# A four-layer transformer kernel: GpSimd's order of square roots and additions in the second layer's recurrence stage

## The chip, the cores and the metric

One core of a Trainium2 chip runs the whole program. The metric is the device time of one execution in microseconds (us). Before the change it is 2499.39 us, the median of 3 runs (2498.11 to 2508.93).

Engines are called PE (TensorE), ACT (ScalarE), DVE (VectorE), Pool (GpSimd) and SP (SyncE, which here only starts transfers). Each works through its own list of instructions in order and waits on semaphores where the list says so.

## What is computed

The reference applies four layers, each an attention-like part and a feed-forward part, to x of 8 sequences (B) of 100 rows (S) of 512 columns (D). The part in question is the attention-like part of the third one in the reference's counting (L2, called "the second layer" in the kernel's names, since two stand ahead of it in L0 and L1 and it has the class `SecondLayer`). Cut to what matters:

```python
# L2_xattn, called with Z = layernorm(x)
states = scan over kv of s = K * s + (kv @ W_in.T + b_in)
summary = mean over the rows of (states @ W_out.T + b_out)     # one vector of 512 per sequence
y = Z + summary
mu, var = mean and variance of y over its last axis
out = (y - mu) / sqrt(var + 1e-5) * gamma + beta
x = x + out
```

After it comes L2's feed-forward part: rows are normalized, rounded to an 8-bit format in blocks of 32, multiplied by gate and up weights, passed through silu, rounded again and multiplied by the down weights.

## The kernel before

The kernel is written engine by engine, in stages with a barrier between them. `stage_L2_recurrence` (L2874 to L3068) is one stage; `stage_ffn` (L2032) follows it as the next. The summaries are already there when the stage begins. The stage has two jobs that share the engines.

**The sequences.** All 8 sequences are held in `res` and are taken in the order 7, 0, 1, ... 6 (`ORDER`), called here by their position i = 0 to 7. For each, DVE does:

- `first(i)`: `measure` of res, that is mean and variance (L2954, L2955) and variance plus epsilon (L2956);
- `shifted(i)`: minus mean times reciprocal root (L2964), which ACT needs for `add_shift(i)` (L2933, summary plus shift);
- `second(i)`: y = res times root plus what ACT made (L2971), then `measure` of y;
- `third(i)`: (y minus mean) times gamma (L2980), then times the second root plus `rb` (L2982), which is the new res.

Pool computes both reciprocal roots of a sequence, `root` (L3021, one column to the power of minus a half), and `rb` = res + beta (L3029, 512 columns), called the addition here. `rb` has two buffers, so the addition for i waits until `third(i - 2)` has read the one it overwrites; that is the wait on `res_made` at L3028.

DVE's order in round i is: second(i), first(i + 2), third(i - 1), shifted(i + 2). After round 4 it also measures the last tile of rows (L2988 to L2990), and after round 5 it rounds that tile (L2995 and the helper `quantize_fp8`, L2007 to L2015). Pool's order is the list `roots`: (0,0), (1,0), then for each i the second root of i and the first root of i + 2; the addition for i comes right behind its first root. The last tile's root (L3032) stands behind the first root of i = 6.

**The weights.** SP loads 16 triples of weights, 768 KB each (L2917), into four buffers; triple t waits until PE has turned triple t - 4. PE transposes each in three banks (L3044) and computes the summaries' broadcasts in between (L3052); ACT copies the three banks out (L2943). ACT's `add_shift` for i = 1 to 7 stands in its list behind the copies of triples 0, 1, 4, 6, 8, 10 and 13 (`ADD_AT`), so ACT can be held by either job. Behind its last triple, SP writes the finished sequences into the tiles of the next stage (`into_tiles`, L1997), each after its `third`; sequence 7 (i = 0) goes out between triples 7 and 8.

At the end PE transposes the last tile (L3066), and after the barrier the feed-forward stage starts with that tile's gate and up products (L2134).

Of the kernel before, what the change touches and what calls it, by code (L numbers as in the profile page):

```python
# [12 lines left out]
ALU = mybir.AluOpType  # L13
# [4 lines left out]
B, S, D = 8, 100, 512  # L18
# [26 lines left out]
class Core:  # L45
# [22 lines left out]
    def sb(self, name, shape, dt=F32, ctx=None):  # L68
        return (ctx or self.ctx).enter_context(self.nc.sbuf_tensor(name, shape, dt))

    def sem(self, name):
        assert name not in self.names
        self.names.add(name)
        self.stage_sems.append(self.nc.alloc_semaphore(name))
        return self.stage_sems[-1]
# [2798 lines left out]
def stage_L2_recurrence(k, early, wgu, wd, rt, arrived, lead):  # L2874
# [5 lines left out]
    ORDER = [B - 1] + list(range(B - 1))  # L2880
    with ExitStack() as ctx:
        sb = lambda name, shape, dt=F32: k.sb("l2_" + name, shape, dt, ctx)
        sem = lambda name: k.sem("l2_" + name)
        gam, bet = early.gam, early.bet
# [8 lines left out]
        y, rb = [sb("y0", [S, D]), sb("y1", [S, D]), early.spare[5][0:S, :]], [sb(f"rb{i}", [S, D]) for i in range(2)]  # L2893
# [8 lines left out]
        var_made, rstd_made, y_made, rb_made, res_made, stepped = (  # L2902
            sem("var_made"), sem("rstd_made"), sem("y_made"), sem("beta_added"), sem("res_made"), sem("steps"))
# [6 lines left out]
        with nc.Block() as block:  # L2910

            @block.sync
            def _(sp):
                for t in range(2, FC):
                    if t >= 4:
                        sp.wait_ge(turned, 3 * (t - 3))
                    sp.dma_start(tri[t % 4][:], k.rounded[t]).then_inc(tri_in[t % 4], 16)  # L2917
                    if t == B - 1:
                        sp.wait_ge(res_made, 1)
                        into_tiles(k, sp, rt, ORDER[0], arrived)  # L2920
                for i, b in enumerate(ORDER[1:]):
                    sp.wait_ge(res_made, i + 2)
                    into_tiles(k, sp, rt, b, arrived)
# [93 lines left out]
            @block.gpsimd  # L3017
            def _(pool):

                def root(n):  # L3020
                    pool.tensor_tensor(rstd[:, n:n + 1], var[:, n:n + 1], k.half[0:S, :], ALU.pow).then_inc(rstd_made, 1)  # L3021

                for at, (i, which) in enumerate(roots):
                    pool.wait_ge(var_made, at + 1)
                    root(2 * i + which)
                    if which == 0:
                        if i >= 2:
                            pool.wait_ge(res_made, i - 1)  # L3028
                        pool.tensor_tensor(rb[i % 2][:], k.res[:, ORDER[i], :], bet[:], ALU.add).then_inc(rb_made, 1)  # L3029
                    if (i, which) == (B - 2, 0):  # L3030
                        pool.wait_ge(x_var_made, 1)
                        pool.tensor_tensor(x_rstd[:], x_var[:], k.half[0:m_last, :], ALU.pow).then_inc(x_rstd_made, 1)  # L3032

            @block.tensor
            def _(pe):
# [35 lines left out]
def stage_L2(k, early, third, weights):  # L3071

    with ExitStack() as ctx:
        wgu = k.sb("s2_wgu", [P, KC, 2 * FF], F32, ctx)
        wd = k.sb("s2_wd", [P, FC, D], F32, ctx)
        rt = k.sb("s2_rows", [P, len(TILES), D], F32, ctx)
        arrived = [k.sem(f"s2_tile{t}") for t in range(len(TILES))]
        third_in = k.sem("s2_third_in")
        lead = k.sb("s2_lead", [P, 1, KC, P], F32, ctx)
        stage_L2_recurrence(k, early, wgu, wd, rt, arrived, lead)  # L3080

        def prefetch(sp):
            for dst, src in zip([third.last, *early.kv, third.ctx[:]], weights):
                sp.dma_start(dst, src).then_inc(third_in, 16)
            return (third_in, 6 * 16),

        stage_ffn(k, "f2", wgu[:, :, 0:FF], wgu[:, :, FF:2 * FF], wd[:], rt,
                  [(a, 16 * len(tile_pieces(t))) for t, a in enumerate(arrived)], quantize_fp8, BLOCK, begin=prefetch, lead=lead[:])
# [847 lines left out]
```

## Time and profile before

| what | value |
|---|---|
| median of 3 runs | 2499.39 us |
| the profiled execution, its own time | 2497.65 us |
| its span | 2495.9 us |
| PE busy | 2368.1 us (95%) |
| DVE busy | 1345.6 us (54%) |
| ACT busy | 786.3 us (32%) |
| Pool busy | 729.7 us (29%) |
| stage_L2_recurrence, about | 1591 to 1652 us of the span |

Times in the views count from the start of the span. A start and a duration stand first; what is in square brackets is the time that the engine stood idle before the instruction, and what ended it. The shares of the whole span say little about a stage of 61 us: each engine's waits have to be read from the stage's own window.

### The profile page before, as it was taken

The numbers are of one execution on the slowest core, as the hardware profiler recorded it, in microseconds if no ns is written. First come the engines' busy times: TensorE is split into PE (matmuls) and PEld (weight loads), VectorE is DVE, ScalarE is ACT, GpSimd is POOL, SyncE is SP. The second block draws the span as 40 slices with busy tenths as digits, with TensorE's granted clock in tenths as the row PEclk, the third lists the DMA queues.
The fourth block names the chain that finished last, engine by engine and source line by source line (L and its number), as shares of the span: only waits on it lengthen the run. The fifth ranks groups of instructions, "written<-read, shape, count | busy, mean of one in ns | idle before, by whom it ended". The sixth has DMA issues, their size and how long they took to land. (4 is left out here: it accounts for less than half of the span.)

```text
span 2495.9 us, 30147 instructions
## 1 busy us (share of the span) xinstructions
PE 2368.1 (95%) x10329; PEld 1276.0 (51%) x10329; DVE 1345.6 (54%) x3448; ACT 786.3 (32%) x2069; POOL 729.7 (29%) x728
## 2 busy tenths in 40 slices
PE   8999999989999998999979999879999899999899
PEld 4455455556355555555555555534444344444454
DVE  5544344126111324767667777676664355565797
ACT  1134444204011113555541010321110255655433
POOL 3655455204100004311133334310000165665200
PEclk9999999999999998999959999989999899999799
DMA  7026200014285543110043222530000321210100
GB/s 192 1 80 218 88 17 8 0 46 141 81 293 206 194 142 87 51 35 30 1 154 132 98 82 99 207 140 6 4 9 4 111 58 47 55 47 28 37 13 15
DMA packets 93678, 203.31 MB, mean 81 GB/s; under 512 B 18580, under 2 KB 37428, under 8 KB 91864
## 3 DMA queue, kind: packets, MB, share of 16 engines
q1 hardware_dynamic: 87384, 188.26, 22.5%
q0 software_dynamic: 6144, 13.13, 1.9%
q8 instruction: 85, 1.39, 0.2%
q14 instruction: 65, 0.53, 0.1%
HBM read 150.45 MB, written 45.94 MB: 79 GB/s over the span
## 5 line engine op out<-in xcount | busy, mean ns | idle before, releaser
L3638 POOL TENSOR_SCALAR a_p<-a_p,a_li 100x257 f32<-100x257 f32 x252 | 188.4, 771 | 110.3 <-DVE a_li L3501 110.3
L633 POOL TENSOR_SCALAR a_shared<-a_shared,a_li 128x361 f32<-128x361 f32 x104 | 131.8, 1267 | 182.3 <-DVE a_li L541 182.3
L3256 PE MATMUL bank<-l_early,a_ctx 128*128 128x512 f32 (+1 forms) x384 | 180.0, 614 | 0.0
L2560 PE MATMUL bank<-s_xT,s_w 128*128 128x400 f32 x512 | 179.0, 504 | 0.8 <-PEq L2757 0.8
L2560 PEld LDWEIGHTS bank<-s_xT,s_w 128*128 128x128 f32 x512 | 98.1, 192 | 77.1 <-issue 3.9
L1853 POOL DMA_INDIRECT a_got<-slots_y,slots_of x32 | 33.8, 1057 | 318.6 <-POOLq L1193 309.8
L3256 PEld LDWEIGHTS bank<-l_early,a_ctx 128*128 128x128 f32 (+1 forms) x384 | 68.8, 188 | 85.0 <-issue 84.9
L313 PE MATMUL bank<-a_wk,a_ctx 128*128 128x512 f32 (+1 forms) x192 | 95.2, 616 | 9.7 <-DMA a_wk<-in_L_xattn_Wk 6.1
L691 ACT ACTIVATE a_shared<-a_shared,a_nm 128x361 f32<-128x361 f32 x104 | 62.1, 597 | 99.5 <-DVE a_nm L535 99.5
L2355 ACT ACTIVATE f_sg<-bank 128x512 f32<-128x512 f32 x25 | 14.9, 597 | 241.4 <-PE bank L2138 221.7
L2570 PE MATMUL bank<-f_h,s_w 128*128 128x400 f32 x256 | 90.9, 499 | 0.0
L313 PE MATMUL bank<-a_wv,a_ctx 128*128 128x512 f32 (+1 forms) x192 | 90.7, 592 | 0.0
L2629 ACT ACTIVATE f_sg<-bank 128x400 f32<-128x400 f32 x32 | 16.1, 504 | 236.2 <-PE bank L2560 236.2
L396 PE MATMUL bank<-a_q_o,a_wq_wo 128*128 128x400 f32 x256 | 88.4, 500 | 0.6 <-issue 0.6
L1284 PE MATMUL bank<-e_wd,e_midT 128*128 128x512 f32 (+1 forms) x192 | 87.9, 593 | 0.6 <-ACT e_midT L1321 0.6
L2164 PE MATMUL bank<-s_wd,f_hT 128*128 128x512 f32 x192 | 87.1, 598 | 0.0
L1546 PE MATMUL bank<-w_wv,w_ctx 128*128 128x512 f32 (+1 forms) x192 | 87.0, 597 | 0.0
L328 PE MATMUL bank<-a_wq_wo,a_shared 128*128 128x512 f32 x192 | 86.5, 593 | 0.0
L1538 PE MATMUL bank<-w_ctx,w_wk 128*128 128x361 f32 x256 | 86.1, 480 | 0.0
L2138 PE MATMUL bank<-s_wgu,f_xT 128*128 128x512 f32 x192 | 84.6, 593 | 0.7 <-ACTq L2345 0.7
L2138 PE MATMUL bank<-s_wgu,s_lead 128*128 128x512 f32 x192 | 84.4, 592 | 0.0
L1341 DVE TENSOR_TENSOR e_mid<-e_sg,bank 128x352 f32<-128x352 f32 x32 | 16.7, 521 | 125.1 <-PE bank L1264 125.1
(477 smaller groups left out, 4964.3 us busy)
## 6 DMA issues: line engine op xcount, KB each, us to landing
slots_x<-zero SPq DMA_DIRECT2D x4, 4096.0 KB, 27.0
f_triple<-in_L_ffn_triples SPq DMA_DIRECT2D x16, 768.0 KB, 4.3
rounded<-f_triple SPq DMA_DIRECT2D x16, 768.0 KB, 3.3
s_whole<-in_L_ffn_w SPq DMA_DIRECT2D x24, 512.0 KB, 3.7
e_wg<-in_L_ffn_w_gate SPq DMA_DIRECT2D x16, 704.0 KB, 4.5
e_wu<-in_L_ffn_w_up SPq DMA_DIRECT2D x16, 704.0 KB, 6.5
e_wd<-in_L_ffn_w_down SPq DMA_DIRECT2D x16, 512.0 KB, 4.1
e_xg<-slots_x SPq DMA_DIRECT2D x16, 512.0 KB, 5.3
```

What stands on the lines that cost most here:

```text
L313: mm = nc.tensor.matmul(R.bank(name, b, c)[0:m, :], cx[:, kc, lo:lo + m], w[:, kc, :], start=(kc == 0), stop=(kc == KC - 1))
L328: mm = nc.tensor.matmul(bank[:], xnT[:, kc, t * P:(t + 1) * P], wq[:, kc, n * D:(n + 1) * D], start=(kc == 0), stop=(kc == KC - 1))
L396: mm = nc.tensor.matmul(R.bank("y", half, m)[:, 0:BY_HALF * S], wo[:, h, m * P:(m + 1) * P], qo[:, half * BY_HALF:(half + 1) * BY_HALF, h, ...
L633: pool.tensor_scalar(p[s % NP], p[s % NP], li[:, b % 2, h:h + 1], None, ALU.mult).then_inc(normed, 1)
L1284: mm = nc.tensor.matmul(b_y[:], midT[u % 2][0:n, c, :], wd[e % 2][0:n, c, :], start=(c == 0), stop=(c == len(IC) - 1))
L1546: mm = nc.tensor.matmul(R.bank("v", b, c)[0:m, :], cx[b % 2][:, kc, lo:lo + m], wvs[:, kc, :], start=(kc == 0), stop=(kc == KC - 1))
L2138: mm = nc.tensor.matmul(banks[u % 2][:], xT[i % 2][:, n, kc, :], w[:, kc, j * D:(j + 1) * D], start=(kc == 0 and n == 0), stop=(kc == KC - ...
L2164: mm = nc.tensor.matmul(b_y[i % 2][:], hT[u % 2][:, n, kc, :], down[:, j * KC + kc, :], start=(j == 0 and kc == 0 and n == 0), stop=(j == ...
L2560: mm = nc.tensor.matmul(banks[f % 2][:, 0:GT], w[:, kc, f * P:(f + 1) * P], xT[:, kc, :], start=(kc == 0), stop=(kc == KC - 1))
L2570: mm = nc.tensor.matmul(b_y[d][:, 0:GT], down[:, f, d * P:(d + 1) * P], h[f % 2][:], start=(f == 0), stop=(f == FC - 1))
L3256: mm = nc.tensor.matmul(bank[0:m, :], columns[:, kc], w[:, kc, :], start=(kc == 0), stop=(kc == KC - 1))
L3638: pool.tensor_scalar(p[g % 2][j][:, lo:hi], p[g % 2][j][:, lo:hi], li[:, h, i:i + 1], None, ALU.mult) \
```

## The change

Pool now takes the second root of i and the first root of i + 2 one after the other, and only then does an addition: the one for i + 1 instead of i + 2. The first two additions stay where they were; the last one stands between the two last roots. The additions, their waits and the number of instructions stay the same.

```diff
+                def add_beta(i):
+                    if i >= 2:
+                        pool.wait_ge(res_made, i - 1)
+                    pool.tensor_tensor(rb[i % 2][:], k.res[:, ORDER[i], :], bet[:], ALU.add).then_inc(rb_made, 1)
+
                 for at, (i, which) in enumerate(roots):
                     pool.wait_ge(var_made, at + 1)
                     root(2 * i + which)
-                    if which == 0:
-                        if i >= 2:
-                            pool.wait_ge(res_made, i - 1)
-                        pool.tensor_tensor(rb[i % 2][:], k.res[:, ORDER[i], :], bet[:], ALU.add).then_inc(rb_made, 1)
+                    if which == 0 and i < 2:
+                        add_beta(i)
+                    elif which == 0 and i >= 3:
+                        add_beta(i - 1)
                     if (i, which) == (B - 2, 0):
                         pool.wait_ge(x_var_made, 1)
                         pool.tensor_tensor(x_rstd[:], x_var[:], k.half[0:m_last, :], ALU.pow).then_inc(x_rstd_made, 1)
+                    if (i, which) == (B - 2, 1):
+                        add_beta(B - 1)
```

## Rows read from the trace of the kernel before

**Rows 1.** The page, part 1: busy time of each engine over the span.
```profile
PE 2368.1 (95%) x10329; PEld 1276.0 (51%) x10329; DVE 1345.6 (54%) x3448; ACT 786.3 (32%) x2069; POOL 729.7 (29%) x728
```

**Rows 2.** Waits from 1588 to 1668: who waited for whom, total, times, longest.
```profile
POOL l_rb L3029 <- DVE res L2982: 32.5, 6, 8.9
...
DVE l_shift L2964 <- POOL l_rstd L3021: 13.2, 6, 2.9
```

**Rows 3.** DVE's timeline in the recurrence stage: start, duration, engine, line, operation.
```profile
1595.52 1.52 DVE L2971 SCALAR_TENSOR_TENSOR l_y<-res,l_rstd,l_early 100x512 f32<-100x512 f32 x1 [0.76 <-ACT l_early L2933]
...
1603.56 0.75 DVE L2982 SCALAR_TENSOR_TENSOR res<-l_y,l_rstd,l_rb 100x512 f32<-100x512 f32 x1
1606.73 0.16 DVE L2964 SCALAR_TENSOR_TENSOR l_shift<-l_stat,l_rstd 100x1 f32<-100x1 f32 x1 [2.42 <-POOL l_rstd L3021]
1606.81 0.74 DVE L2971 SCALAR_TENSOR_TENSOR l_early<-res,l_rstd,l_early 100x512 f32<-100x512 f32 x1
...
1610.39 0.75 DVE L2982 SCALAR_TENSOR_TENSOR res<-l_y,l_rstd,l_rb 100x512 f32<-100x512 f32 x1
...
1627.23 0.67 DVE L2988 BATCH_NORM_STATS2 l_x_stats<-s_rows 32x6 f32<-32x512 f32 x1
...
1628.21 0.73 DVE L2971 SCALAR_TENSOR_TENSOR l_early<-res,l_rstd,l_early 100x512 f32<-100x512 f32 x1
...
1635.44 0.16 DVE L2964 SCALAR_TENSOR_TENSOR l_shift<-l_stat,l_rstd 100x1 f32<-100x1 f32 x1 [2.91 <-POOL l_rstd L3021]
...
1643.46 0.75 DVE L2982 SCALAR_TENSOR_TENSOR res<-l_early,l_rstd,l_rb 100x512 f32<-100x512 f32 x1
1644.13 0.75 DVE L2971 SCALAR_TENSOR_TENSOR l_y<-res,l_rstd,l_early 100x512 f32<-100x512 f32 x1
...
1645.86 0.15 DVE L2956 TENSOR_SCALAR l_var<-l_stat 100x1 f32<-100x1 f32 x1
1646.54 0.75 DVE L2980 SCALAR_TENSOR_TENSOR l_y<-l_y,l_stat,l_early 100x512 f32<-100x512 f32 x1 [0.53 <-POOL l_rstd L3021]
...
1648.78 0.75 DVE L2982 SCALAR_TENSOR_TENSOR res<-l_y,l_rstd,l_rb 100x512 f32<-100x512 f32 x1
```

**Rows 4.** Pool's timeline in the same stage.
```profile
1595.23 1.26 POOL L3029 TENSOR_TENSOR l_rb<-res,l_early 100x512 f32<-100x512 f32 x1
...
1604.39 1.28 POOL L3029 TENSOR_TENSOR l_rb<-res,l_early 100x512 f32<-100x512 f32 x1 [4.52 <-DVE res L2982]
1605.62 1.07 POOL L3021 TENSOR_TENSOR l_rstd<-l_var,half 100x1 f32<-100x1 f32 x2
...
1644.30 1.70 POOL L3029 TENSOR_TENSOR l_rb<-res,l_early 100x512 f32<-100x512 f32 x1 [8.89 <-DVE res L2982]
```

**Rows 5.** ACT's timeline: the last copy of triple 8, and add_shift(5).
```profile
1617.89 0.60 ACT L2943 COPY s_wd<-bank 128x512 f32<-128x512 f32 x1
...
1620.54 0.69 ACT L2933 ACTIVATE l_early<-bank,l_shift 100x512 f32<-100x512 f32 x1 [2.05 <-DVE l_shift L2964]
```

**Rows 6.** PE's timeline: triple 8, and the next stage's first products.
```profile
1616.23 1.53 PE L3044 MATMUL bank<-ident,l_early 128*128 128x128 f32 x12 [2.28 <-DMA l_early<-rounded]
...
1652.07 9.37 PE L2134 MATMUL bank<-s_wgu,s_lead 128*32 128x512 f32 x64 [10.61 <-PEq L2910]
```

**Rows 7.** Five us in mid-stage: PE, PEld, DVE, ACT, POOL busy, PEclk, DMA share, GB/s.
```profile
1615.00:1620.00 5.00, 3.77 (x26) 2.82 (x27) 2.78 (x8) 2.44 (x5) 1.97 (x3) 1.00 1.01 381
```

**Rows 8.** SP's timeline: finished sequences into the tiles of the next stage.
```profile
1625.80 25.48 SPq L1997 DMA_DIRECT2D s_rows<-res  x12
```

**Rows 9.** The third layer's timeline, Pool's root beside DVE's products.
```profile
1974.73 0.74 POOL L3651 TENSOR_TENSOR a_rstd<-a_var,half 100x1 f32<-100x1 f32 x1
...
1974.32 2.33 DVE L3477 SCALAR_TENSOR_TENSOR a_k<-a_k,a_kr,a_nk 128x512 f32<-128x512 f32 x3 [0.17 <-POOL a_kr L3643]
```

**Rows 10.** The next stage's first products in two windows: PE, PEld busy, PEclk, DMA share, GB/s.
```profile
1652.07:1656.70 4.63, 4.63 (x24) 1.33 (x28) 0.50 0.73 242
1656.70:1661.40 4.70, 4.70 (x44) 1.22 (x36) 1.00 1.01 427
```

## The prediction

> **What bounds the kernel now.** I read the shares first: PE is busy 95% of the span [rows 1], so over the whole kernel time is won by shortening stretches in which PE isn't. The recurrence stage is one: ahead of the next stage's first products PE stood idle 10.61 us [rows 6]. What PE waits for there is the stage's end, so I read next who waits inside the stage. Two entries of the list of waits form a ring [rows 2]: Pool waited 32.5 us in six pieces for DVE's finished res before its additions, and DVE waited 13.2 us in six pieces for Pool's roots before the shift. The timelines show the ring turning. DVE starts the last product of a sequence at 1603.56 and ends it at about 1604.31; Pool's addition starts at 1604.39, 0.08 later, and behind it stand two roots, 1605.62 and on for 1.07; only when the second is done does DVE go on, at 1606.73, after 2.42 us idle [rows 3, 4]. The inputs of both roots were there before the addition began: Pool's own order held them up. The same pattern stands four times with 2.40 to 2.42, once with 2.91 (at 1635.44, where the last tile's root stands in Pool's list too), and the first of the six waits, 13.2 - 2.91 - 4 x 2.4 = 0.7, is ahead of the ring and stays. From res of the last sequence (1648.78 + 0.75 = 1649.53) to the next stage (1652.07) it is 2.54 us [rows 3, 6], in which SP sends the last pieces [rows 8]. So DVE's chain ends the stage.
>
> **The change part by part.** No instruction is added or removed. Three things move.
>
> *Both roots ahead of the addition, rounds 1 to 5.* The inputs come before third(i - 1), which takes DVE 0.75 + 0.75 with its gaps; two roots take 1.07 [rows 4], the first of them a good 0.9 earlier than the second. So both are ready when DVE reaches the shift and its wait goes to nothing. Without a wait, DVE starts the next instruction 0.67 after the start of the last product (1643.46 to 1644.13), and second follows the shift by 0.08 [rows 3]. A round from second to the last product takes 3.58 (1606.81 to 1610.39), so a round costs 3.58 + 0.67 + 0.08 = 4.33 instead of 6.81. Pool's work in a round is 1.26 + 1.07 = 2.33 and fits [rows 4].
>
> Starting from 1603.56: shift at 1604.23, second(2) at 1604.31, second(3) at 1608.64, second(4) at 1612.97. Round 4 ends with the measurement of the last tile, 1628.21 - 1627.23 = 0.98 [rows 3], so second(5) would start at 1612.97 + 4.33 + 0.98 = 1618.28.
>
> *What is late next.* second(5) needs add_shift(5), which ACT has behind the copies of triple 8. PE waited for that triple's transfer until 1616.23 [rows 6], and there the DMA engines were busy throughout (share 1.01) [rows 7], so it won't come earlier. ACT's last copy of it starts at 1617.89; a next instruction follows after about 0.47 us, at 1618.36, and add_shift takes 0.69 [rows 5], so second(5) starts at about 1619.08. That is a new wait of 0.8 us. Before, it started at 1628.21: gained so far 9.13.
>
> *Rounds 5 to 7.* The wait of 2.91 before the shift goes, with 0.07 for the restart: 2.98. The rounding of the last tile, second(6) and third(5) cost what they did. Then, at 1646.54, DVE waited for the second root of i = 6, because Pool had the last addition ahead of it [rows 3, 4]. Now that root is done before. Third(6) can start right behind the variance op, 0.07 after 1645.86, instead of at 1646.54: gained 0.61. The last addition now stands between the two last roots. It takes 1.70 from 0.09 after res, as it does now, and ends about when the last variance is there, so it costs nothing; third(6)'s 1.5 us of products cover the last root.
>
> *The queues passed.* Pool issues no DMA in this stage. SP's transfers of finished sequences stand behind the last triple in its list whatever Pool does [rows 8]; four sequences will be done by then instead of three to four, and SP needs some 0.8 us for each piece, done by about 1630, ahead of the last three sequences. The tail of 2.54 stays.
>
> *Collisions.* Before, five of the additions in the ring ran while DVE stood idle. Now each runs beside second. The trace shows both outcomes. At 1644.30 an addition came 0.17 after the start of second: DVE kept its 0.75 and the addition took 1.70 instead of 1.26. At 1595.52 second came 0.29 after an addition had started and took 1.52 instead of 0.75 [rows 3, 4]. In the new rounds second starts 0.09 ahead of the addition (at the end of res; Pool follows 0.08 or 0.09 later). That is on the side of the first case, so I take nothing for DVE; the upper bound is 1.2 in each of rounds 1, 2, 3 and 5 (DVE held to the addition's end, as at 1595.52, where it ended 1.81 after Pool's start instead of 0.65), less the 0.8 that the new wait would swallow. The Trainium skill, SBUF — State Buffer, "SBUF: two separate sides", speaks against this change: a GpSimd instruction and a VectorE instruction with two SBUF inputs share a port pair under an exclusive lock, and whichever starts first holds it for its whole instruction. By it the sum stays if VectorE counts as first, and falls by the upper bound if GpSimd does; the two stretched rows agree with it.
>
> The root of i + 2 now runs beside third's products. Beside three such products back to back (2.33 us together, so none was stretched) a root took 0.74 instead of some 0.55 [rows 9]. The root slips between two of them: 0.2 later, covered by the second product. In round 5 the addition meets the first instructions of the rounding: bounds 0 and one addition, 1.26; I take 0.1, since small one-input instructions beside an addition, such as the one at 1645.86, keep their 0.15.
>
> *The next stage.* It starts after idle time of PE in both kernels, at a granted clock of 0.50, that is 1.2 GHz, for 4.63 us, then 2.4 GHz [rows 10]. The idle time ahead shrinks (some 7 instead of 10.61 us), so it may start otherwise. Bounds: half of 4.63 less, or half clock also over the second window, 4.70 more. I take no difference, the row itself.
>
> **Sum:** 9.13 + 2.98 + 0.61 - 0.1 = 12.6 us. Against the profiled execution's 2497.65 that makes 2485.0; the median of the runs is 1.7 above it, so 2499.39 - 12.6 = 2486.8. A measurement of this kernel can tell about 0.5% from no change, 12.5 us: the forecast lies on that line.
>
> **The rivals.**
>
> *A, collisions go Pool's way.* Price as above: rounds 1 to 3 lose 3 x 1.16 - 0.8 = 2.7, round 5 about 0.7; gain 9.2, time 2490.2. For it: the margin is only 0.09 us, and DVE's instruction is then still behind the shift in its pipe. Against: the order of the starts. The skill's lock, cited above, is the same mechanism.
>
> *B, the stream of weights becomes the bound.* ACT's add_shift waits behind copies of triples that arrive no faster; if the copies slip by another 1.5 us around triples 8 to 10, or triple 13's by as much, the wait of 0.8 grows to 2.3: gain 11.1, time 2488.3. For it: the DMA share of 1.01 [rows 7]. Against: those transfers are asked for at the same times as before.
>
> *C, the change doesn't do what it says.* If the second root were starved by third's products and the shift still came after the addition, nothing would be won: 2499.4. Rows 9 speak against it.
>
> *D, slower.* If Pool's addition and roots held DVE's second and both products of third, each for a whole addition, a round would lose 3 x 1.26 = 3.8 and win 2.5: five rounds 6.5 us more, 2505.9. It decides from 2.5 us lost a round. The largest stretch in these rows is 0.77 for one instruction.
>
> **How the numbers follow.** Forecast 0.68, A 0.20, B 0.08, C 0.02, D 0.02. The forecast's own range is 2485 to 2488 (1 us for the next stage's clock, 1 for the measurement). The range 2484.3 to 2490.9 adds A and B. Faster by over 0.5% is a little over half of the forecast's share, for a clock that can also give: 0.40. D's price is under 0.5%, slower by over 0.5% gets 0.01; the rest, 0.59, is within 0.5%.
>
> **What would show it.** DVE's waits for l_rstd before the shift: only the first (0.7) left; second(2), (3), (4) 4.33 apart; second(5) behind ACT at about 1619.1 with a wait of 0.8 on l_early; Pool's additions 1.70 to 1.8 long in rounds 1 to 3 with second at 0.75 (under A: additions 1.26 and second 1.5 to 1.9); roots of 0.7 beside third; PE's first products of the next stage at about 1639.5. It is wrong if the rounds are over 5 us apart, if that start comes after 1643, or if it comes there and the kernel's time doesn't follow.

## The result, and the profile after

The changed kernel took 2494.24 us in the median of 12 runs (2486.83 to 2496.72), the kernel before beside it 2500.41 us (12 runs). The ratio is 0.9965, 95% interval 0.9954 to 0.9977: 8.7 us of 2500, faster, but less than the 12.6 forecast, and the median lies outside the range given. Measured twice more, beside other kernels, the changed kernel came to 2490.43 us (0.9954, 0.9940 to 0.9967) and 2490.82 us (0.9960, 0.9946 to 0.9973).

The stage itself shows what the change did without the noise of the rest. From DVE's first instruction in it (the copy into `l_each`, at 1591.32 before) to the next stage's first product (1652.07, [rows 6]) it took 60.75 us. In the changed kernel's profile it runs from 1595.21 to 1649.04: 53.83 us, a gain of 6.92 where 12.6 was forecast. The profiled execution's own time fell from 2497.65 to 2495.03 only, because the preceding feed-forward part was 3.6 us longer in this execution. That part is untouched by the change and took 276 to 277 or 280 to 281 us from one execution to the next, of either kernel. The thirteen profiled executions with the longer time had a stretch of 6.8 us in it at a granted clock of 0.50 (here from 1449.4 to 1456.2), the five with the shorter one had none.

Who waited, 1580 to 1660, after the change. These rows answer to [rows 2]:

```profile
POOL l_rstd L3021 <- DVE l_var L2956: 27.9, 12, 7.2
...
DVE l_y L2971 <- ACT l_early L2933: 4.6, 2, 3.8
...
POOL l_rb L3026 <- DVE res L2982: 2.8, 6, 0.5
...
DVE l_early L2971 <- ACT l_early L2933: 2.4, 1, 2.4
...
DVE l_shift L2964 <- POOL l_rstd L3021: 0.7, 1, 0.7
```

The ring is open. DVE's 13.2 us for Pool's roots are down to the 0.7 that the prediction left standing, and Pool's 32.5 us for res to 2.8. In their place DVE waits for ACT: 3.8 and 2.4 us for `add_shift`, and 0.8 at the start, which stood before too [rows 3].

DVE's timeline after; compare [rows 3]:

```profile
1607.45 0.75 DVE L2982 SCALAR_TENSOR_TENSOR res<-l_y,l_rstd,l_rb 100x512 f32<-100x512 f32 x1
1608.12 0.15 DVE L2964 SCALAR_TENSOR_TENSOR l_shift<-l_stat,l_rstd 100x1 f32<-100x1 f32 x1
1608.19 0.74 DVE L2971 SCALAR_TENSOR_TENSOR l_early<-res,l_rstd,l_early 100x512 f32<-100x512 f32 x1
...
1612.44 0.15 DVE L2964 SCALAR_TENSOR_TENSOR l_shift<-l_stat,l_rstd 100x1 f32<-100x1 f32 x1
1616.39 0.75 DVE L2971 SCALAR_TENSOR_TENSOR l_y<-res,l_rstd,l_early 100x512 f32<-100x512 f32 x1 [3.80 <-ACT l_early L2933]
...
1620.71 0.74 DVE L2971 SCALAR_TENSOR_TENSOR l_y<-res,l_rstd,l_early 100x512 f32<-100x512 f32 x1
...
1628.50 0.75 DVE L2971 SCALAR_TENSOR_TENSOR l_early<-res,l_rstd,l_early 100x512 f32<-100x512 f32 x1 [2.42 <-ACT l_early L2933]
...
1634.10 0.42 DVE L2008 TENSOR_SCALAR l_x_top<-l_x_top 32x16 f32<-32x16 f32 x1
...
1645.73 0.75 DVE L2982 SCALAR_TENSOR_TENSOR res<-l_y,l_rstd,l_rb 100x512 f32<-100x512 f32 x1
```

A round without a wait is 4.32 us (shift to shift, 1608.12 to 1612.44) and the restart is 0.67, as forecast. second(3) then stands from 1612.5 to 1616.39, and second(5) until 1628.50.

Pool's timeline, one round of it; compare [rows 4]:

```profile
1606.84 0.99 POOL L3021 TENSOR_TENSOR l_rstd<-l_var,half 100x1 f32<-100x1 f32 x1 [0.46 <-DVE l_var L2956]
1608.29 1.77 POOL L3026 TENSOR_TENSOR l_rb<-res,l_early 100x512 f32<-100x512 f32 x1 [0.46 <-DVE res L2982]
1610.15 0.55 POOL L3021 TENSOR_TENSOR l_rstd<-l_var,half 100x1 f32<-100x1 f32 x1
```

Pool now pays for the collisions (its instructions that overlap DVE's), out of time that it has. The root beside third's products takes 0.99 instead of 0.55 and is still done before the shift; the addition beside second takes 1.77, and second keeps its 0.74.

PE's timeline shows what ACT waits for, and the windows under it the clock (their columns are PE, PEld, DVE, ACT, POOL busy, PEclk, DMA share, GB/s):

```profile
1608.61 5.08 PE L3051 MATMUL bank<-ident,l_triple 128*128 128x128 f32 x24
...
1622.92 2.82 PE L3051 MATMUL bank<-ident,l_early 128*128 128x128 f32 x12 [0.78 <-DMA l_early<-rounded]
1625.67 2.02 PE L3059 MATMUL bank<-l_summaries,l_each 8*100 8x512 f32 x2
```
```profile
1596.30:1613.20 16.90, 16.90 (x54) 10.82 (x53) 14.15 (x36) 7.75 (x14) 10.06 (x12) 0.50 0.54 191
1613.30:1620.00 6.70, 5.95 (x45) 4.62 (x44) 3.40 (x9) 6.55 (x13) 1.76 (x3) 1.00 0.95 295
1620.20:1630.20 10.00, 9.22 (x36) 6.94 (x35) 7.23 (x18) 5.36 (x9) 5.22 (x6) 0.50 0.90 352
```

For 17 us from the stage's start the granted clock was 0.50 (1.2 GHz), with PE busy every one of them, and again for 10 us from 1620. Twelve transposes of one triple, 1.53 us at full clock [rows 6], took 2.82, and a summary's products 2.02 instead of 1.10. In the kernel before's profile the clock was back at 1.00 7.4 us after the stage's start. So triple 4, behind which add_shift(3) stands in ACT's list, was laid out after 1615; triple 8, behind which add_shift(5) stands, was turned from 1622.92 instead of 1616.23, 27.7 us into the stage instead of 24.9.

The last thing that ACT waited for ahead of add_shift(5) was not a copy, though, but the summary's product behind triple 8 (1625.67 + 2.02 = 1627.69). ACT's row after, and PE's row of that product in the kernel before:

```profile
1627.78 0.69 ACT L2933 ACTIVATE l_early<-bank,l_shift 100x512 f32<-100x512 f32 x1 [1.42 <-PE bank L3059]
```
```profile
1617.69 1.10 PE L3052 MATMUL bank<-l_summaries,l_each 8*100 8x512 f32 x2
```

The transfers moved too. SP asked for triple 8 at 1606.72 before, 15.4 us into the stage, and at 1615.52 after, 20.3 us into it:

```profile
1606.72 1.52 SPq L2917 DMA_DIRECT2D l_early<-rounded  x2
```
```profile
1615.52 1.20 SPq L2917 DMA_DIRECT2D l_early<-rounded  x2
```

That is one execution. Two theories can be made of it. Theory 1: the stream of weights through PE and ACT is the new bound, and how much it takes back hangs on what the clock happens to do. Theory 2: the stage always gives 7 us and the forecast missed a fixed cost.

### The profile page after: what moved, and what is told of

Its sections match the earlier page's. It is cut to its first block and busy times, and to the rows that moved or that the text cites. A ratio compares the mean times of both kernels' runs of the same rounds, so it can differ in the third digit from the quotient of the medians.

```text
span 2493.3 us, 30147 instructions
## 1 busy us (share of the span) xinstructions
PE 2377.4 (95%) x10329; PEld 1284.9 (52%) x10329; DVE 1345.9 (54%) x3448; ACT 786.8 (32%) x2069; POOL 733.4 (29%) x728
## 3 DMA queue, kind: packets, MB, share of 16 engines
q8 instruction: 85, 1.39, 0.2%
```

## The experiments

Stages are measured as above, in the one profiled execution of each run. "Half clock" is how long the granted clock stood at 0.50 after it fell at the stage's start.

**e1, e11, e15: the changed kernel again, three more executions.**

> The changed kernel once more. In the first look its recurrence stage (from DVE's first instruction to the next stage's first product) took 53.8 us against 60.8 before, with PE at half clock from 1596.5 to 1613.6, and DVE waited 3.8 and 2.4 us for add_shift. Theory 1 (the stream of weights through PE and ACT is the new bound, and how late it is hangs on when PE's granted clock is 0.5): another execution shows another pattern of half clock, and the stage's length follows it: near 48 us where the clock is full early, 52 to 56 where it is half for 10 us or more; ratio 0.995 to 0.998. Theory 2 (the stage always gives 7 us, the rest never existed because of collisions of Pool and DVE): 53.8 within 0.3 us whatever the clock does, second over 0.75 us long somewhere.

> The changed kernel a third time, for one more pair of clock pattern and stage length. Theory 1: half clock for 10 us at the start gives 50.0 as in the second look, 17 us gives 53.8 as in the first, 7 us gives 48.4 to 49.5.

> The changed kernel a fourth time, on the same chip as the two others, as their measure: ratio 0.995 to 0.9970, stage 48.5, 50.0 or 53.8 us for 6.8, 10.2 or 17.1 us of half clock at its start.

| profiled execution of the changed kernel | half clock | second stretch of it | second(3), second(5) waited | stage |
|---|---|---|---|---|
| first | 17 us | 10 us | 3.80, 2.42 | 53.83 |
| e15 | 13.6 us | 10 us | 2.21, 4.08 | 53.89 |
| e1 | 10.2 us | 3.4 us | 0.74, 1.38 | 50.04 |
| e11 | 6.8 us | 3.4 us | none, 1.00 | 48.50 |

The wait of second(5) in DVE's timeline, e11 and then e15:

```profile
1622.01 0.75 DVE L2971 SCALAR_TENSOR_TENSOR l_early<-res,l_rstd,l_early 100x512 f32<-100x512 f32 x1 [1.00 <-ACT l_early L2933]
```
```profile
1627.45 0.75 DVE L2971 SCALAR_TENSOR_TENSOR l_early<-res,l_rstd,l_early 100x512 f32<-100x512 f32 x1 [4.08 <-ACT l_early L2933]
```

and the windows of e11's and of e15's clock (columns as above):

```profile
1594.60:1601.20 6.60, 6.55 (x17) 3.53 (x18) 5.60 (x13) 1.89 (x4) 3.76 (x5) 0.50 0.60 240
1601.40:1614.90 13.50, 11.48 (x78) 8.28 (x77) 12.15 (x32) 11.68 (x23) 8.47 (x10) 1.00 0.83 276
```
```profile
1596.00:1609.40 13.40, 13.40 (x43) 8.40 (x42) 11.43 (x28) 6.65 (x11) 8.04 (x10) 0.50 0.59 220
...
1619.90:1629.90 10.00, 8.43 (x32) 6.16 (x31) 5.64 (x14) 5.10 (x9) 3.79 (x5) 0.50 0.76 300
```

The stage's length follows the clock from execution to execution over 5.4 us; theory 2 is out. Without the two waits the four stages are alike: 47.61, 47.60, 47.92 and 47.50 us in the table's order, and 0.33 of e1's 47.92 is a second(3) of 1.08 us instead of 0.75 beside an addition. The clock at the start also moves the request for triple 8: 20.3, 18.6, 17.0 and 15.4 us into the stage. The expectations named only the first stretch and gave 48.5, 50.0 or 53.8 for it; e15 shows that the second counts too: 13.6 us of the first and 10 of the second gave as much as 17 and 10. With the clock early at full, as it was in the profile that the forecast was made from, the stage was 48.50 where 60.75 - 12.6 = 48.15 was forecast. The mean over the four stages is a gain of 9.2 us; the three ratios are 8.7, 11.5 and 10.0 us.

**e2: the kernel before again.**

> The kernel before once more, for a second look at its stage. Theory 1: Pool's wait of 2.4 us a round gives the stream of weights slack, so the stage stays at 60 to 62 us even where PE's clock is half for longer than in the first look, and the waits of DVE for the root stay 2.4. Theory 2 says the same of the length.

2501.61 us, and a stage of 60.75 us, the same to 0.01, with half clock for 17 us:

```profile
1596.00:1612.90 16.90, 16.90 (x58) 11.59 (x57) 12.46 (x31) 8.77 (x15) 6.88 (x9) 0.50 0.59 210
```
```profile
POOL l_rb L3029 <- DVE res L2982: 32.5, 6, 8.9
...
DVE l_shift L2964 <- POOL l_rstd L3021: 13.2, 6, 2.9
```

The waits are those of [rows 2] to the last digit. The 2.4 us that DVE lost to Pool in each round were slack for the weights, enough for either clock. This is why the profile before couldn't show how the stream does when nothing gives it slack.

**e4: PE's share of the stream cut.** Only the first of four blocks of each part is transposed; the other columns of the weights are what the bank held.

```diff
-                        for kc in range(KC):
+                        for kc in range(1):
```

> The changed kernel, but PE transposes only the first of the four 128-column blocks of each part of a triple; the other three parts of the weights are left as the bank held them, so this leaves out three quarters of the transposes. Theory 1: PE's clock no longer matters to the stage, only the transfers do: no wait for add_shift over 1 us, stage 47.5 to 49 us, that is the forecast's 12.6 us; ratio 0.994 to 0.996. Theory 2: stage 53 to 54 us still. A third, that the transfers alone are the bound (share 1.01 in mid-stage): stage 52 to 54 us too, but with DVE's waits on add_shift kept while PE waits for DMA.

Stage 47.58 us; ratio 0.9931 (0.9913 to 0.9949). DVE never waited for add_shift after the first, though the clock was at half for all of it:

```profile
1597.70:1643.70 46.00, 30.15 (x67) 11.50 (x65) 40.12 (x91) 29.00 (x57) 25.07 (x25) 0.50 0.78 271
```

So the clock matters to the stage through PE's transposes. All transfers are still there in e4, and PE could start on triple 8 at 1618.30, 22.1 us into the stage, where e11 had 24.6: the transfers by themselves don't make DVE wait either.

**e10: no transfers of triples 4 to 15.** What they would bring is left out of the weights.

```diff
-                    sp.dma_start(tri[t % 4][:], k.rounded[t]).then_inc(tri_in[t % 4], 16)
+                    if t < 4:
+                        sp.dma_start(tri[t % 4][:], k.rounded[t]).then_inc(tri_in[t % 4], 16)
...
-                    if t >= 2:
+                    if 2 <= t < 4:
                         pe.wait_ge(tri_in[t % 4], 16 * (t // 4 + (t % 4 >= 2)))
```

> The changed kernel without the transfers of triples 4 to 15; PE turns what the buffers hold already, so the wrong weights are laid out and this leaves out three quarters of the loading. If transfers alone delay add_shift: no wait of DVE for it, 47.6. If PE and ACT at half clock do: waits of 0.5 to 3.5 us stay, stage 49 to 52, longer the longer the clock is half. With the clock full early: 47.6.

Half clock was 6.8 us here, as in e11, and the stage 47.69 us against e11's 48.50, with no wait of DVE for add_shift but the one at the start. Beside e11, the transfers cost 0.8 us. But it takes both jobs to make that wait, since e4, with all transfers and a quarter of the transposes, hasn't got it either: a triple is asked for when PE has turned the one four before it. The two executions also differ in the clock, which fell a second time at 20.9 us into e11's stage and not before 38.2 us in e10's. e10 was profiled once, with a short stretch of half clock; what the transfers cost with a long one stays open.

**e3: add_shift one triple earlier.**

```diff
-        ADD_AT = [0, 1, 4, 6, 8, 10, 13]
+        ADD_AT = [0, 1, 3, 5, 7, 9, 12]
...
-                    elif t >= 6 and t % 2 == 0 and t // 2 + 1 < B:
-                        summary(t // 2 + 1)
+                    elif t >= 5 and t % 2 == 1 and (t + 3) // 2 < B:
+                        summary((t + 3) // 2)
```

> The changed kernel with ACT's add_shift for i = 3 to 7 behind triples 3, 5, 7, 9, 12 instead of 4, 6, 8, 10, 13, and the summaries' products on PE moved along. Theory 1: DVE's waits for add_shift fall by a triple each, some 2 us for the one behind triple 4, nearly all of the others; stage 49 to 52 us; 1 to 4 us faster than the changed kernel, ratio to before 0.9945 to 0.997. Theory 2: stage and time as the changed kernel's, ratio 0.9965.

2488.68 us, ratio 0.9946 (0.9932 to 0.9960), beside e1's 0.9954. The stage was 47.60 us, under the 49 to 52 expected, with 10.2 us of half clock; e1 had the same clock at the start and 50.04. Both waits of DVE are gone. e3's clock didn't fall a second time before 45.8 us into the stage, as e1's did for 3.4 us, but that isn't what saved them: PE came to triple 8 at 26.3 us into the stage in e3 and at 26.2 in e1. What was new is that add_shift(5) no longer stood behind it:

```profile
1622.21 0.92 DVE L2971 SCALAR_TENSOR_TENSOR l_early<-res,l_rstd,l_early 100x512 f32<-100x512 f32 x1
```

**e7: the same edit on the kernel before.**

> The kernel before with ACT's add_shift one triple earlier, the edit that took the changed kernel's stage from 50.0 to 47.6. Theory 1: before the change DVE never waited for add_shift in these rounds, since Pool held it longer, so nothing moves: stage 60.75 within 0.1, ratio 0.999 to 1.001. Rival: the edit helps by itself, 58 to 60.

Stage 60.73 us with 17 us of half clock, ratio 1.0004 (0.9995 to 1.0013): nothing. What costs 2.4 us in the changed kernel (e1 beside e3, one execution each) cost nothing in the one before. The position of add_shift became a bound by the change.

**e6: the last addition's part alone.**

```diff
-                    if which == 0:
-                        if i >= 2:
-                            pool.wait_ge(res_made, i - 1)
-                        pool.tensor_tensor(rb[i % 2][:], k.res[:, ORDER[i], :], bet[:], ALU.add).then_inc(rb_made, 1)
+                    if (which == 0 and i < B - 1) or (i, which) == (B - 2, 1):
+                        n = i if which == 0 else B - 1
+                        if n >= 2:
+                            pool.wait_ge(res_made, n - 1)
+                        pool.tensor_tensor(rb[n % 2][:], k.res[:, ORDER[n], :], bet[:], ALU.add).then_inc(rb_made, 1)
```

> The kernel before with one part of the change alone: the addition for i = 7 stands behind the second root of i = 6. Forecast for this part: 0.61 us of the stage's 60.75, so 60.1; DVE's wait of 0.53 ahead of third(6) gone, the five waits of 2.4 to 2.9 left. Rival: 60.75 still, because the second root of i = 7 comes late in its place.

60.12 us: 0.63 for the 0.61 of the sum.

**e5: the order left, a third buffer instead.**

```diff
-[sb(f"rb{i}", [S, D]) for i in range(2)]
+[sb(f"rb{i}", [S, D]) for i in range(3)]
...
-                        if i >= 2:
-                            pool.wait_ge(res_made, i - 1)
-                        pool.tensor_tensor(rb[i % 2][:], k.res[:, ORDER[i], :], bet[:], ALU.add).then_inc(rb_made, 1)
+                        if i >= 3:
+                            pool.wait_ge(res_made, i - 2)
+                        pool.tensor_tensor(rb[i % 3][:], k.res[:, ORDER[i], :], bet[:], ALU.add).then_inc(rb_made, 1)
```

> The kernel before in its own order, but with three buffers for res + beta instead of two, so that the addition for i waits for third(i - 3) and not third(i - 2). If the wait of the addition on the finished res is the cause, and the order only a way around it: DVE's waits for l_rstd in rounds 1 to 5 go to nothing here too, stage 48 to 52 us as far as add_shift lets it, ratio 0.994 to 0.997, like the changed kernel. If the order itself matters (roots behind an addition of 1.26 us, and collisions with third), some 0.5 to 1 us a round stays.

Stage 49.96 us with half clock for 10.2 us and then 3.4 more, where e1 had the same and 50.04; ratio 0.9967 (0.9954 to 0.9980). The wait on a finished res in front of the roots was the cause; the order is one way around it, a buffer another. Only the start differs, where an addition came before a shift:

```profile
1603.87 1.22 DVE L2964 SCALAR_TENSOR_TENSOR l_shift<-l_stat,l_rstd 100x1 f32<-100x1 f32 x1 [0.66 <-POOL l_rstd L3021]
```

**e8 and e16: additions where DVE runs only statistics.** With e3's edit; Pool's loop becomes

```diff
+                    if which == 1 and 1 <= i < B - 1:
+                        pool.wait_ge(y_made, i + 1)
+                        add_beta(i - 1 if i < B - 3 else i)
                     pool.wait_ge(var_made, at + 1)
                     root(2 * i + which)
-                    if which == 0 and i < 2:
-                        add_beta(i)
-                    elif which == 0 and i >= 3:
-                        add_beta(i - 1)
                     if (i, which) == (B - 2, 0):
+                        pool.wait_ge(res_made, B - 4)
+                        add_beta(B - 4)
```

> The changed kernel with the earlier add_shift (47.60 us of stage) and the additions placed where DVE runs only statistics: each behind second (a wait on y_made) instead of behind the first roots or third. If a port held by one engine at a time explains the stretched instructions (shift(0) 0.95 instead of 0.15, second(0) 1.52 instead of 0.75, the small scaling 0.43 instead of 0.16, second(5) 0.92 instead of 0.75), all of them fall to the short values: 0.8 + 0.77 + 0.27 + 0.17 = 2.0 less, stage 45.6; ratio 0.993 to 0.995. If the long values have another cause (first use of a tile, ACT's output arriving), they stay and the stage is 47.6 or longer.

> e8's kernel again on the same chip: is its gain over the changed kernel (stage 47.05 against 48.5 to 53.8) seen in the whole time? Expected ratio 0.9935 to 0.9955, 1 to 5 us under the changed kernel; stage 46 to 48 whatever the clock does, since add_shift stands a triple earlier.

The long instructions at the start became short, as the port theory says. e8's timeline of DVE, compare 1595.52 in [rows 3]:

```profile
1594.22 0.15 DVE L2964 SCALAR_TENSOR_TENSOR l_shift<-l_stat,l_rstd 100x1 f32<-100x1 f32 x1
1595.13 0.75 DVE L2971 SCALAR_TENSOR_TENSOR l_y<-res,l_rstd,l_early 100x512 f32<-100x512 f32 x1 [0.76 <-ACT l_early L2933]
...
1599.59 0.75 DVE L2971 SCALAR_TENSOR_TENSOR l_y<-res,l_rstd,l_early 100x512 f32<-100x512 f32 x1 [0.68 <-ACT l_early L2933]
```

The small scaling fell to 0.16 too; only second(5), beside the addition left in round 4, kept 0.92. Yet the stage was 47.05 and 47.07 us, 0.5 less than e3's and not 2.0: the third row above shows the won time turning into waits for add_shift again (0.68 and 0.30 in e8, 1.10 in e16), early in the stage where PE is at half clock in every execution. In the whole time: 2488.97 us, 0.9952 (0.9935 to 0.9968), and 2487.87 us, 0.9949 (0.9934 to 0.9963), beside e15's 0.9960; 3 us of median, and the intervals overlap.

**e9: a real product ahead of each triple.**

```diff
+                        if i == 0:
+                            nc.tensor.matmul(t_bank[n % 4][:], k.ident[:], k.zero[:], start=True, stop=True)
```

> The changed kernel with one real product ahead of each triple's transposes: the identity times 512 columns of zeros into the bank that the transposes then overwrite. It adds 16 products to PE. So far the clock stayed at 0.50 for 10 to 17 us at the start of the stage although PE was busy all the time with transposes. Theory 1: if products and not transposes bring the clock to 1.00, the half-clock stretch ends after some 7 us, DVE's waits for add_shift fall to what the transfers leave (0.8 as forecast, up to 1.4), stage 48.4 to 49.5 us, that is the forecast's 48.1 and 0.26 for the one collision seen. Rival: PE is only loaded further and the clock does as before, stage 50 to 54.

The clock was at half for 6.8 us and then at full for 44, with no second stretch, which the changed kernel had in all four executions:

```profile
1603.50:1647.70 44.20, 39.92 (x226) 26.39 (x224) 36.71 (x78) 28.05 (x54) 19.06 (x19) 1.00 0.75 248
```

The added product isn't shown to be what kept it there: without one, and with add_shift a triple earlier, e3, e8 and e16 had no second stretch for 34 to 38 us either. And the stage was 53.41 us all the same. The expectation had left out the price, which PE's timeline shows:

```profile
1609.78 1.02 PE L3051 MATMUL bank<-zero,ident 128*128 128x512 f32 x2
1610.64 1.47 PE L3053 MATMUL bank<-ident,l_triple 128*128 128x128 f32 x12
```

A triple took PE 2.17 us (1609.78 to 1611.95) instead of 1.4, and PE was the bound at full clock too. Ratio 0.9968 (0.9954 to 0.9982).

**e13: the product ahead of the first two triples only.**

```diff
+                        if i == 0 and t < 2:
```

> The changed kernel with the added product of zeros ahead of the first two triples alone. e9, with 16 of them, had its clock at 0.50 for only 6.8 us, but 1.0 us more PE work a triple made PE the bound (53.4). If products at the start are what ends the half-clock stretch early, it is 6.8 us here too, and with 14 products less the stage is 48.5 to 50, the two products costing up to 2 us each at half clock ahead of triples 0 and 1. If it was chance in e9 and e12, 10 or 17 us of half clock can come again, with 50 to 56.

Half clock 6.8 us again; stage 50.44, above the 48.5 to 50 expected, ratio 0.9956 (0.9939 to 0.9973). The products, at half clock themselves, hold triples 0 and 1, and second(1) waits 0.48 for it. Another 0.44 of waiting at second(3) let Pool's addition come first, and second took 1.39 instead of 0.75. second(5) waited 1.23 for add_shift, with the clock at full from 8.5 to 42.6 us into the stage.

**e12 and e14: all edits together,** e8's kernel with the product ahead of all 16 triples and ahead of two.

> The kernel of e8 (earlier add_shift, additions beside statistics) with the products of e9. e8's stage was 47.05, with waits of 0.76, 0.68 and 0.30 for add_shift at its start. If these are PE at half clock, the later two go and the stage is 46.0 to 46.5; ratio 0.9925 to 0.9955, at or below any other here. If the added products delay the summaries more than the clock gives back, 47 or more.

> e8's kernel (earlier add_shift, additions beside statistics) with the product ahead of the first two triples. Stage 46 to 48.5 us: e8's 47.05 with 0.68 + 0.30 of waits to win, and up to 2 us of product in front of triple 1. Ratio 0.9925 to 0.9955.

Ratios 0.9938 (0.9926 to 0.9950), 2486.31 us, and 0.9936 (0.9922 to 0.9949), 2485.32 us: the two lowest ratios of kernels that compute everything, e14 5.5 us of median under the changed kernel on the same chip. Their stages don't explain that: 50.56 and 48.33 us, longer than e8's 47.05. What else they win, if it is not chance, stays open. In both, second(1) waited 2.3 us for add_shift(1) behind the added products.

Half clock at the start was 6.8 us in all four executions with an added product, but also in e10, e11, e16 and the first of the kernel before, which have none. The records show what else goes with it. In those four without a product the clock fell 0.45 to 0.72 us after the stage's start; in the other ten without one it fell 0.96 to 1.79 us after it and stayed down for 10 us or more. Three of the four with a product fell late too (1.20 to 1.63) and yet had 6.8 us. So the products seem to matter where the fall is late. Three executions don't settle it, and no run here shows why.

## Why the prediction was right and wrong

- **The ring of Pool and DVE, rounds 1 to 5:** right in mechanism and size. DVE's waits for the shift went from 13.2 us to 0.7, rounds without a wait are 4.32 us (4.33 forecast), and e5 reaches the same stage by a buffer.
- **Rounds 5 to 7, the last addition:** right, 0.63 us alone (0.61).
- **The queues passed and the tail:** right. From the last res (1645.73 + 0.75 = 1646.48) to the next stage (1649.04) it is 2.56 us (2.54), although SP came to its last 12 pieces only 39.4 us into the stage, later than the "done by about 1630" of the prediction (38.7).
- **The next stage's first products:** right, with no difference taken: 9.61 us after and 9.37 before.
- **Collisions:** the side was right, rival A is out. Where they started on time, second(2), second(3) and second(4) kept 0.74 to 0.75 (all three in e11), in the first execution 0.09 to 0.10 ahead of the addition. A second that came after the addition had begun was stretched: 1.08 for second(3) in e1, and 0.92 for second(5) in e3, e10 and e8, where it didn't wait and the addition of round 4 runs while DVE measures the last tile. The prediction had no term for round 4; in the changed kernel second(5) waited in all four executions, and it cost nothing. By the lock of the Trainium skill, "SBUF — State Buffer", section "SBUF: two separate sides", whichever of the two engines starts first keeps the port pair; the trace agrees in both directions: the addition took 1.77 when second was first, the shift 1.22 in e5 when the addition was. Two sizes were off: the root beside third takes 0.99, not 0.7 (covered), and the small scaling in round 5 0.42 instead of 0.16, so 0.26 us where 0.1 was taken.
- **What is late next:** this is the step that failed. The prediction placed it rightly (DVE behind add_shift behind a triple) and sized it at 0.8 us, at second(5) alone, from ACT's and PE's rows of one execution, whose clock was at full from 7.4 to 38.1 us into the stage. The runs showed 1.00 us (e11), 0.74 + 1.38 (e1), 3.80 + 2.42 (the first) and 2.21 + 4.08 (e15): 1.0 to 6.3 us, by PE's clock in that execution. The prediction asked what the clock does to the next stage's first products and gave that bounds, but not what it does to the transposes inside this one. By its own sign of being wrong, a next stage later than 1643, that is 51.7 us into the stage, two of the four executions fail and two pass.
- **The 0.8 itself:** nearly right with the clock early at full, and partly by luck. The prediction let add_shift(5) start behind ACT's last copy, at 1618.36. It also needs the summary's product, which PE ended at 1617.69 + 1.10 = 1618.79 before and behind which ACT started 0.08 to 0.09 us later in all four executions after: a term of 0.5 us that the prediction left out. In e11 triple 8 came 0.3 us earlier than before (24.6 against 24.9 us into the stage), and the wait was 1.00. In e13, whose clock was at full there too, it was 1.23. That and the small scaling (0.26 for 0.1) make up the 0.35 us between 48.50 and 48.15.
- **Rival B** was the right one: the stream of weights became the bound. It was priced at 1.5 us of slip, for 2488.3, and given 0.08 with the reason that the transfers are asked for at the same times as before. They are not: triple t is asked for when PE has turned triple t - 4, so PE's clock moves the transfers too, for triple 8 from 15.4 to 20.3 us into the stage. And e4 shows that it takes PE's transposes, not the arrival by itself, to make DVE wait.
- **The 0.5% line:** with 6.9 to 12.3 us of stage to gain from one execution to another, within 0.5% was the right side, for another reason than the one given.

## What to carry to other kernels

A wait that is taken away was slack for everything beside it. Before pricing what is late next from its rows, ask what else in those rows could have been different while that wait covered it: here PE's clock, which the stage hid to the hundredth of a microsecond before the change and passed on for up to 5.4 us after it. Where engines share a list with another job (`add_shift` behind copies), the place in the list has to move when the pace does: one triple earlier was worth nothing before and 2.4 us after, in the executions that can be compared. A gain that hangs on what the clock does can't be read from one profile: the changed kernel's first showed 6.9 us of it, its third 12.3.

## What the runs showed of the hardware

- PE busy throughout (99% or more) with transposes and a few summary products kept the granted clock at 0.50 for 6.8 to 17 us at the stage's start, in executions of one and the same kernel. With the transposes cut to a quarter and PE busy two thirds of the time it stayed there for 51 us, past the stage's end. With a product of 512 columns ahead of each triple it then stayed at 1.00 for 44 us, and without one for up to 37.6 us (e16).
- The length of that first stretch is not set by the program alone: 7, 10, 14 and 17 us in the four executions of the changed kernel, 7 and 17 in the two of the one before. Without an added product it was 6.8 us where the clock fell within 0.72 us of the stage's start and 10 us or more where it fell later.
- A one-column root on Pool takes 0.55 us alone and 0.99 when it starts 0.16 us into the first of two products of DVE, which keep their 0.74 and 0.75. A 512-column addition that starts first holds a 0.15 us instruction of DVE to 0.95 or 1.22.
